# One transformer layer on one core: the last two value projections run among the first scores, probability buffers are numbered anew, and VectorE's third tile is taken at position 12

## The chip, the cores and the metric

The kernel runs on 1 core of one Trainium2 chip. The metric is the device time in microseconds of one execution. The times of the kernel before are 620.38 us median of 3 runs (620.07 to 620.94).

## What is computed

One layer in float32 on 2048 tokens of 256 channels: self-attention with 16 heads of 16 channels, a residual and a layer norm, then a gated feed-forward part with int8 weights, a residual and a second layer norm. Cut to what matters:

```python
Q = X @ Wq + bq; K = X @ Wk + bk; V = X @ Wv + bv           # 2048 x 256 each
scores = einsum('bhqd,bhkd->bhqk', q, k) / sqrt(16)         # 16 heads
attn = softmax(scores); out = einsum('bhqk,bhkd->bhqd', attn, v)
x = layernorm(X + out @ Wo + bo)
ffn = qmatmul(silu(qmatmul(x, w_gate, s_gate)) * qmatmul(x, w_up, s_up), w_down, s_down)
x = layernorm(x + ffn)
```

## The kernel before, in words

Every engine has its own hand-written list of instructions, and semaphores tie the lists together. Projections are done in three products of "high" and "low" parts, so that the result has nearly float32 precision.

**Projections.** TensorE (PE) turns X in four chunks of 512 tokens, projects queries and keys (`QK`, 16 tiles), and then values: `project_v(p)` for p = 0 to 7, each 12 matmuls of 256 columns for 256 tokens, into the PSUM bank `V_BANK[p]`. VectorE (DVE) copies each to `v_all` with the bias added (`save_v`, line 716). On its list `write_bound(0)` and `write_bound(1)` (line 737) stand among the eight `save_v`, and behind them the load of `exact_flag` (line 747) and a branch round a general path which these inputs don't need. PE (line 1129) and SyncE (SP, line 453) have the same load and branch.

**Attention** goes in 16 steps (4 chunks of 512 queries times 4 groups of 4 heads), each of 16 units, one for 128 keys. In unit u, PE runs `scores(2u)` and `scores(2u+1)` (line 1190: two matmuls each, 512 columns), and then `prob_times_v(u-2)` (line 1216: four matmuls, one for each head), so products run two units behind scores. Score pairs go round three pairs of PSUM banks, so `scores(g)` waits for the exponential of pair g-3. ScalarE (ACT) takes each pair as one exponential of 1024 columns (line 629) into `probs`, six buffers in turn (`g % HALVES`).

**Tiles taken by VectorE.** In a step, for some key tiles `kt` the exponential of head 0 is done by DVE with a polynomial (`exponentials`, lines 852 to 876, eight instructions), and ACT then takes only 512 columns of that pair. They are tiles 10 and 13 in step 1, and 2, 6, 10 and 13 in steps 2 to 15 (`poly_tiles`). Since DVE takes longer, head 0 multiplies such a tile later: `value_order` sets for each position of a step which tile head 0 takes there, while heads 1 to 3 take the tile of the position. Before, tile 10 is taken at position 13, and the ordinary tiles fill the positions between in their order, so that position 12 takes tile 14.

**What stands between.** In steps 5, 6, 9, 10, 13 and 14 PE runs `project_out` (line 1238, four matmuls) behind units 8 and 15; in steps 8 and 12 `turn_y` behind units 3 and 8.

**SP's queue** issues nearly all transfers: inputs, weights (`gate8`, `up8` and `down8` at lines 362 to 364), then `load_queries(0)`, the keys of step 0 (`load_k`), `load_queries(1)`, and `load_keys(1)` to `load_keys(3)` (lines 382, 384 and 392). Behind them come the flag, `load_queries(2)` with `load_shift` (line 406), and `move_out(0)`. DVE's first polynomial waits until the keys of steps 2 and 3 are loaded, since its buffers lie over `k_part`.

**Memory.** `probs` lies over `xt_hi` and the lower half of `xt_lo`, which the value projections read; `w_hi` and `w_lo`, with the value weights in them, lie over the keys of step 2.

Of the kernel before, what the change touches and what calls it, by code (L numbers as in the profile page):

```python
# [7 lines left out]
def layer_program(nc, X, Wq, bq, Wk, bk, Wv, bv, Wo, bo, w_gate, w_up, w_down, s_gate, s_up, s_down, out):  # L8
# [7 lines left out]
    P = 128  # L16
# [39 lines left out]
    with ExitStack() as ctx:  # L56
        arena_at = (nc.sbuf_base + 63) // 64 * 64
# [15 lines left out]
        KB = 1024  # L73

        x_tok = place("x_tok", [P, TT, HID], f32)
        gate8 = place("gate8", [P, KO, INTER // 4], i32)
        up8 = place("up8", [P, KO, INTER // 4], i32)
        down8 = place("down8", [P, MT, HID // 4], i32)
# [56 lines left out]
        w_hi = place("w_hi", [P, 3, KO, HID], f32r, at + 32 * KB)  # L135
        w_lo = place("w_lo", [P, 3, KO, HID], f32r, at + 38 * KB)
# [147 lines left out]
        V_BANK = [4, 5, 2, 3, 4, 5, 7, 6]  # L284
# [23 lines left out]
        def value_order(s):  # L308

            behind = {2: 5, 6: 9, 10: 13, 13: 15}  # L310
            late = {behind[kt]: kt for kt in poly_tiles(s)}
            others = [kt for kt in range(UPS) if kt not in poly_tiles(s)]
            return [late[i] if i in late else others.pop(0) for i in range(UPS)]

# [21 lines left out]
        def _(sp):  # L336
# [25 lines left out]
            sp.dma_start(gate8[:], w_gate.rearrange("(k p) n -> p k n", p=P)).then_inc(late_loaded, 16)  # L362
            sp.dma_start(up8[:], w_up.rearrange("(k p) n -> p k n", p=P)).then_inc(late_loaded, 16)
# [82 lines left out]
            sp.wait_ge(v_psum, TT // 2)  # L446
# [7 lines left out]
            with sp.If(need_exact > 0):  # L454
                sp.wait_ge(q_loaded[0], QUERY)
                for s in range(STEPS):

                    if s:
                        sp.wait_ge(gen_max, s * NQ * TPC + 2)
                    load_queries(s, 0, gen_loaded)  # L460
                sp.wait_ge(gen_max, STEPS * NQ * TPC + 2)
                load_queries(0, 0, gen_reloaded)

                sp.wait_ge(gen_split, 3)
                load_shift(0, 0, gen_reloaded)
# [108 lines left out]
        def _(act):  # L574
# [12 lines left out]
            def hi_of_w(i):  # L587
                act.wait_ge(w_loaded[i], 16)
                nc.scalar.copy(w_hi[:, i, :, :], w_raw[:, i, :].rearrange("p (k n) -> p k n", k=KO)
                               ).then_inc(w_hi_ready, 1)  # L590
# [75 lines left out]
        def _(dve):  # L666
# [14 lines left out]
            def lo_of_w(i):  # L681
                dve.wait_ge(w_hi_ready, i + 1)
                nc.vector.tensor_tensor(w_lo[:, i, :, :], w_raw[:, i, :].rearrange("p (k n) -> p k n", k=KO),
                                        w_hi[:, i, :, :].bitcast(f32), ALU.subtract).then_inc(w_ready, 1)
# [58 lines left out]
            for p in range(3, TT // 2):  # L743
                save_v(p)
# [3 lines left out]
            with dve.If(need_exact > 0):  # L748
# [28 lines left out]
                nc.vector.tensor_copy(shift[:, 1, :], shift_rest[:]).then_inc(gen_split, 1)  # L777

# [251 lines left out]
        def _(pe):  # L1030
# [69 lines left out]
            def project_v(p):  # L1100
# [4 lines left out]
                elif p in (4, 5):  # L1105

                    pe.wait_ge(v_ready, p - 3)
                elif p >= 6:

                    pe.wait_ge(norms_ready, 1)  # L1110
                for a in range(2):
# [4 lines left out]
                                    lambda ko: w_hi[:, 2, ko, :], lambda ko: w_lo[:, 2, ko, :])  # L1116
# [8 lines left out]
            for p in range(1, TT // 2):  # L1125
# [4 lines left out]
            with pe.If(need_exact > 0):  # L1130
# [6 lines left out]
                pe.wait_ge(v_ready, TT // 2)  # L1137
# [26 lines left out]
            def scores(g):  # L1164
# [15 lines left out]
                elif g < 3:  # L1180

                    pe.wait_ge(v_ready, 2 * (g + 1))
# [12 lines left out]
            def prob_times_v(u):  # L1195

                s, kt = u // UPS, u % UPS
                if u == 0:
                    pe.wait_ge(v_ones, 1)
                    pe.wait_ge(v_ready, TT // 2)  # L1200
# [9 lines left out]
                for hh in range(NQ):  # L1210
# [3 lines left out]
                    else:  # L1214
                        prob = probs[:, g % HALVES, hh % 2, :]
# [152 lines left out]
```

## Time and profile before

| | us |
|---|---|
| median of 3 runs | 620.38 (620.07 to 620.94) |
| the profiled execution's own time | 621.71 |
| its span in the trace | 619.9 |
| PE busy | 590.7 (95%) |
| ACT busy | 511.7 (83%) |
| DVE busy | 408.3 (66%) |
| GpSimd busy | 54.6 (9%) |
| mean granted TensorE clock | 0.992 of full |

The attention steps lie between 46.4 us and about 516 us of the span, the projections before them and most of the feed-forward part after them. A busy PE says little by itself: a matmul that is spread out counts as busy. The waits are read from the timeline, where a row in square brackets tells how long its engine stood idle before it and who released it.

### The profile page before, as it was taken

How to read it: one execution, taken by the hardware profiler on the slowest of the kernel's cores; microseconds unless marked ns; L12 is line 12 of the kernel's file. 1: busy time of each engine (PE TensorE's matmuls, PEld its weight loads, DVE VectorE, ACT ScalarE, POOL GpSimd, SP SyncE). 2: the span in 40 equal slices, each digit the busy share in tenths (PEclk: the TensorE clock that was granted, in tenths of full speed). 3: DMA queues.
4: the chain of work that ended last, by engine and by line, in shares of the span. 5: the costliest groups of instructions: out<-in, count | busy, mean ns of one | idle time of the engine just before them, and what ended most of it. 6: DMA issues, size and time to landing. Idle time of an engine off the chain costs nothing.

```text
span 619.9 us, 10436 instructions
## 1 busy us (share of the span) xinstructions
PE 590.7 (95%) x3952; PEld 248.7 (40%) x3952; DVE 408.3 (66%) x748; ACT 511.7 (83%) x614; POOL 54.6 (9%) x51
## 2 busy tenths in 40 slices
PE   8999999999999999999999999999999999999994
PEld 7892222222222222222222222222322226978874
DVE  7672005667676757597775658786766586777875
ACT  4628999999999999999998999999999996253352
POOL 7606000000000000000000000002000001102021
PEclk9997999999999999999999999999999999999998
DMA  9657882211112010101111111102010000101102
GB/s 222 117 94 101 121 107 34 34 27 17 28 13 62 10 30 7 31 7 33 45 30 17 21 22 18 27 11 63 10 30 9 5 7 7 40 1 34 35 1 68
DMA packets 36183, 24.69 MB, mean 40 GB/s; under 512 B 24930, under 2 KB 30946, under 8 KB 35538
## 3 DMA queue, kind: packets, MB, share of 16 engines
q1 hardware_dynamic: 34932, 23.42, 22.3%
q10 hardware_dynamic: 1200, 0.59, 0.4%
q8 instruction: 32, 0.52, 0.3%
q14 instruction: 19, 0.16, 0.1%
HBM read 6.56 MB, written 4.33 MB: 18 GB/s over the span
## 4 chain that ended last, share of the span: by engine, by line
PE 86%; ACT 8%; issue 3%; DVE 2%; DMA 1%; ACTq 0%; POOLq 0%; POOL 0%; DVEq 0%
PE ps L1216 37%; PE ps L1190 25%; PE ps L1321 10%; ACT probs L629 7%; PE ps L1063 5%; PE ps L1298 4%; PE ps L1238 3%; DMA x_tok<-in_L_attn_X 1%; DVE attn_q L784 1%; PE ps L1256 1%; PE ps L1049 1%; DVE stats L1005 0%; DVE r_tmp L1002 0%; DVE xt_lo L689 0%; DVE r_tmp L999 0%
## 5 line engine op out<-in xcount | busy, mean ns | idle before, releaser
L629 ACT ACTIVATE probs<-ps 128x1024 f32<-128x1024 f32 (+1 forms) x512 | 449.1, 1075 | 30.7 <-PE ps L1190 30.7
L1216 PE MATMUL ps<-probs,v_all 128*17 128x512 f32 x1932 | 270.6, 602 | 17.1 <-ACT probs L629 15.8
L1190 PE MATMUL ps<-q_slot,k_stack 51*128 51x512 f32 x1024 | 198.2, 459 | 1.5 <-ACT probs L629 1.5
L1190 PEld LDWEIGHTS ps<-q_slot,k_stack 51*128 51x128 f32 x1024 | 84.3, 185 | 222.7 <-ACT probs L629 209.7
L852 DVE TENSOR_SCALAR bits<-ps 128x512 int32<-128x512 f32 x58 | 40.0, 689 | 61.0 <-PE ps L1190 59.9
L784 DVE COPY attn_q<-ps 128x512 f32<-128x512 f32 x16 | 11.1, 691 | 91.9 <-PE ps L1216 91.9
L1216 PEld LDWEIGHTS ps<-probs,v_all 128*17 128x17 f32 x1932 | 33.6, 95 | 82.6 <-issue 49.0
L648 ACT ACTIVATE sg<-ps,sgate_c 128x512 f32<-128x512 f32 x32 | 22.1, 689 | 49.4 <-PE ps L1321 49.4
L1216 PE MATMUL ps<-poly,v_all 128*17 128x512 f32 x116 | 59.9, 598 | 0.0
L876 DVE SCALAR_TENSOR_TENSOR poly<-poly,bits 128x512 f32<-128x512 f32 x58 | 40.2, 692 | 6.0
L872 DVE SCALAR_TENSOR_TENSOR poly<-poly,mant 128x512 f32<-128x512 f32 x58 | 40.1, 692 | 2.0
L545 POOL TENSOR_TENSOR rstd<-var_eps,minus_half 128x4 f32<-128x4 f32 x4 | 4.1, 1029 | 420.6 <-DVE var_eps L820 420.6
L868 DVE SCALAR_TENSOR_TENSOR poly<-poly 128x512 f32<-128x512 f32 x58 | 39.7, 685 | 0.0
L863 DVE SCALAR_TENSOR_TENSOR poly<-mant 128x512 f32<-128x512 f32 x58 | 39.7, 685 | 0.0
L1321 PE MATMUL ps<-qy,wg 128*128 128x512 f32 x128 | 35.7, 400 | 0.0
L969 DVE SCALAR_TENSOR_TENSOR h<-ps,sup_c,sg 128x512 f32<-128x512 f32 x32 | 23.9, 747 | 16.2 <-ACT sg L648 16.2
L1321 PE MATMUL ps<-qy,wu 128*128 128x512 f32 x128 | 34.4, 390 | 0.0
L1298 PE MATMUL ps<-wd,h_hi 128*128 128x256 f32 x128 | 31.2, 285 | 0.0
L1298 PE MATMUL ps<-wd,h_lo 128*128 128x256 f32 x128 | 30.9, 283 | 0.0
L1321 PEld LDWEIGHTS ps<-qy,wu 128*128 128x128 f32 x128 | 24.0, 188 | 5.4
L858 DVE TENSOR_SCALAR bits<-bits 128x512 int32<-128x512 int32 x58 | 24.8, 428 | 2.0
L866 DVE TENSOR_SCALAR mant<-mant 128x512 f32<-128x512 f32 x58 | 24.8, 427 | 2.0
(97 smaller groups left out, 455.8 us busy)
## 6 DMA issues: line engine op xcount, KB each, us to landing
q_slot<-qy SPq DMA_DIRECT2D x64, 64.0 KB
k_stack<-k_part SPq DMA_DIRECT2D x12, 256.0 KB
at_dram<-attn_q SPq DMA_DIRECT2D x64, 34.0 KB
at<-at_dram SPq DMA_DIRECT2D x8, 272.0 KB, 3.0
q_slot<-qy SPq DMA_DIRECT2D x64, 32.0 KB
x_tok<-in_L_attn_X SPq DMA_DIRECT2D x14, 128.0 KB, 6.3
k_stack<-k_part SPq DMA_DIRECT2D x12, 128.0 KB
out<-out_tmp SPq DMA_DIRECT2D x12, 128.0 KB, 2.2
```

What stands on the lines that cost most here:

```text
L629: nc.scalar.activation(probs[:, g % HALVES, first:2, :].rearrange("p a b -> p (a b)"), ps[:, 2 * ring + first:2 * ring + 2, :].rearrange(" ...
L852: nc.vector.tensor_scalar(bits[:], ps[:, 2 * ring, :], TO_BITS, LOWEST, ALU.mult, ALU.max).then_inc(poly_read, 1)
L858: nc.vector.tensor_scalar(bits[:], bits[:], EXPONENT, BIAS, ALU.bitwise_and, ALU.bitwise_xor).then_inc(poly_exponent, 1)
L863: nc.vector.scalar_tensor_tensor(res, mant_f[:], POLY["a"], mant_f[:], ALU.add, ALU.mult).then_inc(poly_square, 1)
L868: nc.vector.scalar_tensor_tensor(res, res, POLY["b"], res, ALU.add, ALU.mult).then_inc(poly_square, 1)
L872: nc.vector.scalar_tensor_tensor(res, res, POLY["c"], mant_f[:], ALU.add, ALU.mult).then_inc(poly_cube, 1)
L876: nc.vector.scalar_tensor_tensor(res, res, POLY["d"], bits_f[:], ALU.add, ALU.mult).then_inc(poly_done, 1)
L1063: last = nc.tensor.matmul(dst, w(ko), x(ko), start=(n == 0), stop=(n == len(terms) - 1))
L1190: last = nc.tensor.matmul(ps[:, 2 * ring + half, :], k_stack[s % QUADS][base:base + ROWS, p, kt * P:(kt + 1) * P], q_slot[slot][base:base ...
L1216: last = nc.tensor.matmul(ps[32 * hh:32 * hh + VW, ACC, :], v_all[:, tiles[hh], NQ * (s % QUADS) + hh, :], prob, start=(kt == 0), stop=(kt ...
L1298: last = nc.tensor.matmul(ps[:, 4 + i, 0:HID], h[:, m, i * P:(i + 1) * P], wd[:, m, :], start=(m == 0 and j == 0), stop=(m == MT - 1 and j ...
L1321: last = nc.tensor.matmul(ps[:, bank, :], w[:, ko, m * P:(m + 1) * P], qy[:, c, ko, part, :], start=(ko == 0 and part == 0), stop=(ko == K ...
```

## The change

- `project_v(6)` runs between `scores(0)` and `scores(1)`, and `project_v(7)` behind `scores(3)` (the second pair of unit 1). ACT waits for six value projections before its first exponential in place of eight, and for all eight before its fourth (g = 3). `V_BANK` and the waits of the projections are changed to suit.
- DVE does `save_v(6)` and `save_v(7)` behind `write_bound(1)`, the flag and the branch.
- `probs` is used in the order of slots 0, 2, 4, 1, 3, 5, since the rows that `project_v(6)` and `project_v(7)` still read lie under slots 1, 3 and 5.
- The value weights' parts have a place of their own (`wv_hi`, `wv_lo`) over `gate8` and `up8`. These two loads (256 KB each) are moved on SP's queue from line 362 to behind the flag, ahead of `load_queries(2)`. `load_keys(2)` no longer waits for the value projections.
- In `value_order`, tile 10 goes to position 12.

```diff
-        V_BANK = [4, 5, 2, 3, 4, 5, 7, 6]
+        V_BANK = [4, 5, 2, 3, 4, 7, 6, 7]
+        V_LATE = 6
...
-            behind = {2: 5, 6: 9, 10: 13, 13: 15}
+            behind = {2: 5, 6: 9, 10: 12, 13: 15}
...
+        def slot_of(g):
+
+            return (0, 2, 4, 1, 3, 5)[g % HALVES]
...
-            sp.dma_start(gate8[:], w_gate.rearrange("(k p) n -> p k n", p=P)).then_inc(late_loaded, 16)
-            sp.dma_start(up8[:], w_up.rearrange("(k p) n -> p k n", p=P)).then_inc(late_loaded, 16)
...
             load_keys(1)
-            sp.wait_ge(v_psum, TT // 2)
             load_keys(2)
...
+            sp.wait_ge(v_psum, TT // 2)
+            sp.dma_start(gate8[:], w_gate.rearrange("(k p) n -> p k n", p=P)).then_inc(late_loaded, 16)
+            sp.dma_start(up8[:], w_up.rearrange("(k p) n -> p k n", p=P)).then_inc(late_loaded, 16)
             for s in range(STEPS):
...
-            act.wait_ge(v_psum, TT // 2)
+            act.wait_ge(v_psum, V_LATE)
...
                 act.wait_ge(scores_ready, g + 1)
+                if g == 3:
+                    act.wait_ge(v_psum, TT // 2)
...
-                    probs[:, g % HALVES, first:2, :].rearrange("p a b -> p (a b)"),
+                    probs[:, slot_of(g), first:2, :].rearrange("p a b -> p (a b)"),
...
-            for p in range(3, TT // 2):
+            for p in range(3, V_LATE):
                 save_v(p)
...
+            for p in range(V_LATE, TT // 2):
+                save_v(p)
...
-            for p in range(1, TT // 2):
+            for p in range(1, V_LATE):
                 project_v(p)
...
-                    pe.wait_ge(v_ready, 2 * (g + 1))
+                    pe.wait_ge(v_ready, 3 + g)
...
                     pe.wait_ge(v_ones, 1)
+                    pe.wait_ge(v_ready, V_LATE + 1)
+                elif u == 2 * (V_LATE + 1):
                     pe.wait_ge(v_ready, TT // 2)
...
                 scores(2 * u)
+                if u == 0:
+                    project_v(V_LATE)
                 scores(2 * u + 1)
+                if u == 1:
+                    project_v(V_LATE + 1)
```

How the lists of instructions move is shown at three places. The first is PE behind the branch, where `MATMUL ps<-q_slot,k_stack` is half a score pair and `ps<-wv_hi,xt_hi` and the like are the value projections. In the kernel before, the eight projections are over here:

```order
213 L1190 MATMUL ps<-q_slot_103,k_stack_92 128x512 [waits bound_ready,ones_ready,norms_ready,k_loaded0,q_loaded0]
214 L1190 MATMUL ps<-q_slot_103,k_stack_92 128x512
215 L1190 MATMUL ps<-q_slot_103,k_stack_92 128x512 [waits v_ready]
```

In the changed kernel:

```order
199 L1208 MATMUL ps<-q_slot_105,k_stack_94 128x512 [waits bound_ready,ones_ready,norms_ready,k_loaded0,q_loaded0]
200 L1208 MATMUL ps<-q_slot_105,k_stack_94 128x512
201 L1078 MATMUL ps<-wv_hi,xt_hi 128x256 [waits norms_ready]
...
207 L1078 MATMUL ps<-wv_hi,xt_lo 128x256 x2
208 L1208 MATMUL ps<-q_slot_105,k_stack_94 128x512 [waits v_ready]
...
212 L1208 MATMUL ps<-q_slot_105,k_stack_94 128x512 [waits exp_done]
213 L1208 MATMUL ps<-q_slot_105,k_stack_94 128x512
214 L1078 MATMUL ps<-wv_hi,xt_hi 128x256 [waits v_ready]
```

Twelve matmuls of a projection now stand behind the first score pair, and twelve more behind the fourth, which is the first one that waits for an exponential.

The second place is PE at the end of step 1: the product of position 12, the scores of unit 15, the product of position 13 (`poly` is a tile that DVE has done, `probs` one of ACT's). Before:

```order
393 L1216 MATMUL ps<-probs,v_all 17x512 [waits exp_done]
394 L1216 MATMUL ps<-probs,v_all 17x512 x3
395 L1190 MATMUL ps<-q_slot_104,k_stack_93 128x512 [waits exp_done]
...
399 L1216 MATMUL ps<-poly,v_all 17x512 [waits poly_done,exp_done]
400 L1216 MATMUL ps<-probs,v_all 17x512 x3
```

In the changed kernel:

```order
393 L1236 MATMUL ps<-poly,v_all 17x512 [waits poly_done,exp_done]
394 L1236 MATMUL ps<-probs,v_all 17x512 x3
395 L1208 MATMUL ps<-q_slot_106,k_stack_95 128x512 [waits exp_done]
...
399 L1236 MATMUL ps<-probs,v_all 17x512 [waits exp_done]
400 L1236 MATMUL ps<-probs,v_all 17x512 x3
```

DVE's tile and ACT's tile have changed places; the number of matmuls is the same.

The third place is SP's queue ahead of the queries of step 2, in the changed kernel:

```order
216 L460 UNCONDITIONAL_BRANCH [waits gen_reloaded]
217 L475 DMA gate_50<-in_L_ffn_w_gate 128x2x256 [waits v_psum]
218 L476 DMA up_51<-in_L_ffn_w_up 128x2x256
219 L378 DMA q_slot_105<-qy 32x1x512 [waits scores_ready]
```

Before, the load of the queries follows the branch directly, and the two weight loads stand ahead of all queries and keys.

## Rows read from the trace of the kernel before

**Rows 1.** The page's costliest groups, the exponentials: busy, mean ns, idle before

```profile
L629 ACT ACTIVATE probs<-ps 128x1024 f32<-128x1024 f32 (+1 forms) x512 | 449.1, 1075 | 30.7 <-PE ps L1190 30.7
```

**Rows 2.** Timeline of ACT: start us, length us, instructions, idle before and its releaser

```profile
46.96 5.61 ACT L629 ACTIVATE probs<-ps 128x1024 f32<-128x1024 f32 x6 [11.81 <-PE ps L1190]
53.27 1.94 ACT L629 ACTIVATE probs<-ps 128x1024 f32<-128x1024 f32 x2 [0.71 <-PE ps L1190]
56.26 48.77 ACT L629 ACTIVATE probs<-ps 128x1024 f32<-128x1024 f32 x54 [1.05 <-PE ps L1190]
105.69 27.73 ACT L629 ACTIVATE probs<-ps 128x1024 f32<-128x1024 f32 x32 [0.66 <-PE ps L1190]
...
208.82 10.31 ACT L629 ACTIVATE probs<-ps 128x1024 f32<-128x1024 f32 x12 [0.37 <-PE ps L1190]
...
222.50 15.84 ACT L629 ACTIVATE probs<-ps 128x1024 f32<-128x1024 f32 x18 [0.77 <-PE ps L1190]
...
513.00 1.94 ACT L629 ACTIVATE probs<-ps 128x1024 f32<-128x1024 f32 x2 [0.66 <-PE ps L1190]
```

**Rows 3.** Timeline of PE, end of step 1: position 12, scores of units 15 and 16

```profile
104.16 1.05 PE L1216 MATMUL ps<-probs,v_all 128*17 128x512 f32 x8 [1.10 <-ACT probs L629]
105.14 0.73 PE L1190 MATMUL ps<-q_slot,k_stack 51*128 51x512 f32 x4
106.79 0.74 PE L1190 MATMUL ps<-q_slot,k_stack 51*128 51x512 f32 x4
```

**Rows 4.** Timeline of DVE and PE, step 6: tile 10's first and last instruction, position 12

```profile
240.42 0.69 DVE L852 TENSOR_SCALAR bits<-ps 128x512 int32<-128x512 f32 x1 [2.95 <-PE ps L1190]
244.53 0.69 DVE L876 SCALAR_TENSOR_TENSOR poly<-poly,bits 128x512 f32<-128x512 f32 x1
248.15 1.05 PE L1216 MATMUL ps<-probs,v_all 128*17 128x512 f32 x8 [1.02 <-ACT probs L629]
```

**Rows 5.** Timeline of PE: an output projection in step 6

```profile
237.11 1.13 PE L1238 MATMUL ps<-wo,at 128*128 128x256 f32 x4
```

**Rows 6.** Timeline of PE: the first matmuls of `project_v(6)`, the first scores

```profile
43.39 0.40 PE L1063 MATMUL ps<-w_hi,xt_hi 128*128 128x256 f32 x2
46.36 0.96 PE L1190 MATMUL ps<-q_slot,k_stack 51*128 51x512 f32 x6
```

**Rows 7.** Timeline of DVE: `save_v(5)`, `write_bound(1)`, and the first polynomial

```profile
43.59 0.69 DVE L716 TENSOR_TENSOR v_all<-ps,bv_b 128x512 f32<-128x512 f32 x1 [0.16 <-PE ps L1063]
47.07 3.53 DVE L737 TENSOR_SCALAR q_slot<-q_slot,bound_neg 1x1024 fp32r<-1x1024 f32 x2
96.08 0.69 DVE L852 TENSOR_SCALAR bits<-ps 128x512 int32<-128x512 f32 x1 [14.41 <-PE ps L1190]
```

**Rows 8.** Instructions on `exact_flag`: duration ns min/median/max, first and last start us

```profile
L747 DVEq TENSOR_LOAD <-exact_flag x1: 548/548/548, 46.5 to 46.5; - x1
L453 SPq TENSOR_LOAD <-exact_flag x1: 2057/2057/2057, 89.9 to 89.9; - x1
```

**Rows 9.** Windows: us, busy (x instructions) of PE, PEld, DVE, ACT, POOL; granted clock; DMA

```profile
48.00:50.00 2.00, 1.13 (x6) 0.51 (x6) 1.97 (x2) 2.00 (x3) 2.00 (x2) 0.96 0.67 86
50.00:52.00 2.00, 2.00 (x10) 0.31 (x10) 0.61 (x1) 2.00 (x3) 2.00 (x3) 0.50 0.82 86
...
93.00:94.00 1.00, 1.00 (x10) 0.19 (x2) 0.00 (x0) 1.00 (x3) 0.00 (x0) 1.00 0.06 16
```

**Rows 10.** Timeline of SP's queue: a weight, step 0's last keys, step 2's queries and shifts

```profile
13.86 2.93 SPq L362 DMA_DIRECT2D gate<-in_L_ffn_w_gate  x1
...
40.35 0.59 SPq L384 DMA_DIRECT2D k_stack<-k_part  x1
...
92.81 0.61 SPq L371 DMA_DIRECT2D q_slot<-qy  x1
...
97.90 2.54 SPq L406 DMA_DIRECT2D q_slot<-shift  x4
```

**Rows 11.** DMA issues from 39 to 41 us: count, KB each, median us to landing

```profile
k_stack<-k_part SPq DMA_DIRECT2D x2, 32.0 KB, 2.0
```

More of the change, by code:

```diff
@@ L56, in layer_program @@
     with ExitStack() as ctx:
+        KB = 1024
         arena_at = (nc.sbuf_base + 63) // 64 * 64
@@ L71, in region @@
             return at
-        KB = 1024
         x_tok = place("x_tok", [P, TT, HID], f32)
+        at = place_at[0]
         gate8 = place("gate8", [P, KO, INTER // 4], i32)
         up8 = place("up8", [P, KO, INTER // 4], i32)
+        wv_hi = place("wv_hi", [P, KO, HID], f32r, at)
+        wv_lo = place("wv_lo", [P, KO, HID], f32r, at + 2 * KB)
         down8 = place("down8", [P, MT, HID // 4], i32)
@@ L134, in layer_program @@
         squares = place("squares", [P, 4, S], bf16, at + 16 * KB)
-        w_hi = place("w_hi", [P, 3, KO, HID], f32r, at + 32 * KB)
-        w_lo = place("w_lo", [P, 3, KO, HID], f32r, at + 38 * KB)
+        w_hi = place("w_hi", [P, 2, KO, HID], f32r, at + 32 * KB)
+        w_lo = place("w_lo", [P, 2, KO, HID], f32r, at + 36 * KB)
         wg = place("wg", [P, KO, INTER], f32r, at)
@@ L588, in hi_of_w @@
                 act.wait_ge(w_loaded[i], 16)
-                nc.scalar.copy(w_hi[:, i, :, :], w_raw[:, i, :].rearrange("p (k n) -> p k n", k=KO)
+                nc.scalar.copy(w_hi[:, i, :, :] if i < 2 else wv_hi[:], w_raw[:, i, :].rearrange("p (k n) -> p k n", k=KO)
                                ).then_inc(w_hi_ready, 1)
@@ L682, in lo_of_w @@
                 dve.wait_ge(w_hi_ready, i + 1)
-                nc.vector.tensor_tensor(w_lo[:, i, :, :], w_raw[:, i, :].rearrange("p (k n) -> p k n", k=KO),
-                                        w_hi[:, i, :, :].bitcast(f32), ALU.subtract).then_inc(w_ready, 1)
+                hi, lo = (w_hi[:, i, :, :], w_lo[:, i, :, :]) if i < 2 else (wv_hi[:], wv_lo[:])
+                nc.vector.tensor_tensor(lo, w_raw[:, i, :].rearrange("p (k n) -> p k n", k=KO), hi.bitcast(f32),
+                                        ALU.subtract).then_inc(w_ready, 1)
             def lo_of_x(c):
@@ L1104, in project_v @@
                     pe.wait_ge(lo_ready, NQK - 3 + p - 0)
-                elif p in (4, 5):
-                    pe.wait_ge(v_ready, p - 3)
-                elif p >= 6:
+                elif p == 4:
+                    pe.wait_ge(v_ready, 1)
+                elif p in (5, 6):
                     pe.wait_ge(norms_ready, 1)
+                elif p == 7:
+                    pe.wait_ge(v_ready, 6)
                 for a in range(2):
@@ L1115, in project_v @@
                                     lambda ko: xt_lo[:, ko, t * P:(t + 1) * P],
-                                    lambda ko: w_hi[:, 2, ko, :], lambda ko: w_lo[:, 2, ko, :])
+                                    lambda ko: wv_hi[:, ko, :], lambda ko: wv_lo[:, ko, :])
                 last.then_inc(v_psum, 1)
@@ L1136, in _ @@
                     pe.wait_ge(k_loaded[quad], keys_of(quad))
-                pe.wait_ge(v_ready, TT // 2)
+                pe.wait_ge(v_ready, V_LATE)
                 pe.wait_ge(norms_ready, 2)
@@ L1214, in prob_times_v @@
                     else:
-                        prob = probs[:, g % HALVES, hh % 2, :]
+                        prob = probs[:, slot_of(g), hh % 2, :]
                     last = nc.tensor.matmul(ps[32 * hh:32 * hh + VW, ACC, :],
```

## The prediction

> **What bounds the kernel now.** I read the page's costliest groups first. The exponentials on ACT are busy for 449.1 us and idle 30.7 us before them, always for PE's scores [rows 1]. 11.8 us of this is the wait for the first one, so some 19 us of idle time lie inside the attention steps. ACT's timeline shows where [rows 2]: it starts at 46.96, is idle 0.71 and 1.05 us in the first eight exponentials, then runs without a break until 105, and from there has a break of 0.66 us once in each step, 15 times from 105.69 to 513.00. Breaks of 0.77 us follow six of these at once (the one at 222.50 is shown), and six of 0.37 to 0.38 us stand in the middle of a step (208.82). The sum is 1.76 + 9.9 + 4.6 + 2.3, and two of 0.2: 19 us, so nothing is missing.
>
> One exponential takes 0.92 us from start to start: (5.61 - 1.94) / 4 [rows 2]. A step with its four half exponentials keeps ACT for 27.73 us. PE needs 106.79 - 105.14 = 1.65 us a unit [rows 3], 26.4 us for 16. So a step is bound by ACT, and each of its breaks is paid in full, as long as PE can use its 1.3 us of room. In steps with two projections of 1.1 us [rows 5] PE needs 28.6 us, and ACT 27.73 + 0.37 + 0.4 = 28.5 if the large break shrinks to the size of the small one: there the two are level.
>
> **Tile 10 at position 12.** At the end of step 1 PE stands idle 1.10 us before the product of position 12, released by ACT [rows 3]. By the lists it takes tile 14 there for head 0, and the scores of tile 14 were issued immediately ahead of it, in the same unit: it waits for an exponential that has just been asked for. Only behind it come the scores of unit 15 at 105.14, and ACT's break ends at 105.69. With tile 10 there, PE needs only a polynomial. Tile 14 goes to position 13, one unit later, behind scores that wait for the same exponential anyway. The same pattern stands in all 15 steps with polynomials: 15 x 0.66 = **-9.9 us**.
>
> Is tile 10 ready? In step 6 its chain begins at 240.42 and ends at 245.22 [rows 4]. PE came to position 12 at 248.15 - 1.02 = 247.13. That is 1.9 us of room. DVE had been idle 2.95 us before the chain, so nothing pushes it.
>
> A projection behind unit 15 now comes right after the stall and costs ACT 0.77 us, one behind unit 8 has no stall ahead and costs 0.37 [rows 2]. Without the stall both should cost alike: 6 x 0.40 = **-2.4 us**. The bounds are 0 (PE is level with ACT there) and 4.6; I take the row for unit 8, which is the same work in the same steps.
>
> **Projections 6 and 7 among the scores.** Projection 6 starts at 43.39 and scores at 46.36 [rows 6]: two projections take 2.88 us. First scores now start at 43.48, if their data are there. The last keys of step 0 are issued at 40.35 [rows 10] and land 2.0 us later [rows 11], at 42.4: in time by 1.1 us. ACT starts 0.60 us behind the scores, at 44.08. Projection 6 (1.44 us) then stands ahead of the second pair: that pair comes at 45.34, ACT sees it at 45.94, idle 0.94 us. Pairs 2 and 3 follow until 46.6, projection 7 ends at 48.1, and the fourth exponential waits for it: the third ended at 47.8, idle 0.4 us. PE has work without a break until then and ACT is fed with three pairs at once, so the breaks of 0.71 and 1.05 us [rows 2], which came while PE waited and then ran slowly, go. Start: -2.88 + 0.94 + 0.4 - 1.76 = **-3.3 us**.
>
> The clock is part of it. PE was busy 1.13 of 2.00 us in the window at 48, and the next has a granted clock of 0.50, that is 1.2 GHz [rows 9]. The Trainium skill ("TensorE: Matmul & The Clock Gate", Part 1) says that half rate is the default and activity lifts it. The trace agrees with the fall. By that rule alone one may fear that the smaller matmuls and waits of the new start still drop it; this is rival D.
>
> DVE now does `save_v(6)` behind `write_bound(1)`, the flag and the branch, and the first product (about 48.9) waits for it. `save_v(5)` ends at 44.28 [rows 7]. The two bounds took 3.53 us beside GpSimd's additions; now they come before those. At worst 44.28 + 3.53 + 0.69 = 48.5, still in time; the flag's load takes 0.55 us on DVE's queue and was done while the engine was at other work [rows 8]. Even if it stood in line with SP's 2.06 us, the first product would be 1.6 us late, which I keep for the range. The move of `save_v(7)` is free: its first reader is unit 14. Renaming the slots moves no work: **0**, covered by the wait of g = 3 that I have counted.
>
> **The weight loads on SP's queue.** This term goes the other way. SP issues the keys of steps 1 to 3 without a pause and reads the flag at 89.9, in 2.06 us [rows 8]. Queries of step 2 start at 92.81, the last shift is issued at 97.90 + 2.54 = 100.44 [rows 10]. Nothing of this chain starts earlier when attention does. Two issues are put ahead of it; on a quiet queue I price them at 0.61 each, like the query's issue at 92.81 (DMA busy 0.06 in 93 to 94 [rows 9]), so 1.2 us, and the queries land at 101.64 + 2.0 = 103.6. They are wanted earlier: pair 64 went to ACT at 105.69 + 1.84 = 107.53, and now could at 107.53 - 0.66 - 3.3 = 103.57, with scores 0.60 us ahead, at 102.97. Loss: **+0.6 us**. Bounds: 0 and rival B. The gap at the input's end of the queue (13.86) hid behind queries that were not yet wanted, so it gives nothing.
>
> DVE's first polynomial waits for the keys of step 3. DMA engines are quiet from 93.0 [rows 9]; the polynomial began at 96.08 [rows 7] and may now begin at 92.8. This is even, 0 to 0.7 us, and it falls in front of the wait for queries, which would swallow it: 0. Everything behind the attention steps is as before; the weights for GpSimd's casts are wanted hundreds of us later.
>
> **Sum:** -9.9 - 2.4 - 3.3 + 0.6 = -15.0 us. The profiled execution took 621.71 us (span 619.9), 1.3 above the median of 620.38. Against its own time this gives 606.7, and for a median **605.4 us**.
>
> **Rivals.**
>
> - **B, the weight loads hold the queue.** If both issues take 2.93 us, as `gate` did at 13.86 [rows 10], they cost 5.9 and not 1.2: the queries land 4.7 us later and PE waits all of it at the head of step 2. 605.4 + 4.7 = 610.1 us. For it: a full queue has made issues this long. Against: the DMA engines have just gone quiet. The Trainium skill ("Trainium Kernel Development and Optimization", Key Constraints) says that all queues share the same 16 DMA engines and interleave; by that, 512 KB ahead of the queries slow them too. That speaks against the change, and no row of before shows it at this place.
> - **C, the stall only moves to position 13.** Then the 9.9 and 2.4 us stay, and the start alone is won: 620.4 - 2.7 = 617.7 us, and no change within the measurement if the start fails too. Against it: at position 13 PE has already waited for that exponential in the scores of unit 15.
> - **D, the clock falls all the same at the start.** The 1.76 us of breaks come back, the wait for queries goes: -9.9 - 2.4 - 1.5, 606.6 us.
> - **E, slower.** The polynomial of tile 10 isn't ready at position 12. Its price is paid in every step from 1.9 us of lateness on, and the kernel is slower once it is some 3.4 us late. If one more chain of 4.8 us stands ahead of it, PE waits 2.9 us, ACT 2.45 in place of 0.66: 15 x 1.79 - 5.1 = +21.8, 642 us. For it: DVE does norms and copies between the tiles in steps 4 to 15. Against: 2.95 us of idle time ahead of the chain [rows 4].
>
> **Numbers.** The forecast (A) gets 0.75, B 0.10, C 0.05, D 0.06, E 0.03, anything else 0.01. A's own bounds are -0.6 (no wait for queries) and -1.6 more (projections cost less than 0.37) below, +2.4 (no gain there) and +1.6 (late `save_v(6)`) above: 603.2 to 609.4 us. This holds A nearly whole, D, and a B with one long issue, 0.8 in all, and so is the range. Under 0.2% (1.2 us) a measurement of this kernel can't tell from no change. Faster by more: A, B, D and most of C, 0.95; within: the rest of C, 0.02; slower: E, 0.03.
>
> **What would show it.** ACT's first exponential at about 44.1; the breaks of 0.66 us gone from its timeline, a step of 27.8 us in place of 28.4, and those of 0.77 near 0.4; position 12 with `poly` and no wait; granted clock 1.00 from 46 to 58; the queries of step 2 issued from about 94.0, and one PE wait of under 1 us at the head of step 2. The prediction is wrong if a break of over 0.4 us stands in each step behind position 12 or 13, if `gate` and `up` take more than 2 us to issue, or if ACT's ninth exponential (at 56.26 before) starts later than 54.

## The result, and the profile after

The changed kernel takes **605.82 us** (median of 4 runs, 604.9 to 608.15), the kernel before, run beside it on the same chip, 620.66 us (620.07 to 621.45). The ratio is 0.9766 (95% interval 0.9734 to 0.9798). Predicted were 605.4 us and a range of 603.2 to 609.4. The profiled execution took 604.9 us with a span of 603.1; the one of before had a span of 619.9. Between the two profiles lie 16.8 us, between the medians 14.8; the difference between these two numbers is part of what follows. One slow execution of the kernel before, of 708.61 us at a mean granted clock of 0.751, belongs to the third set below and is left out of every comparison.

| | before | after |
|---|---|---|
| span of the profile, us | 619.9 | 603.1 |
| PE busy | 590.7 (95%) | 591.0 (98%) |
| ACT busy | 511.7 | 510.2 |
| exponentials: busy, idle before | 449.1, 30.7 | 447.6, 15.0 |
| first exponential | 46.96 | 44.05 |
| granted TensorE clock | 0.992 | 0.998 |

The page's group of exponentials after the change (busy, mean ns, idle before), which answers to [rows 1]:

```profile
L640 ACT ACTIVATE probs<-ps 128x1024 f32<-128x1024 f32 (+1 forms) x512 | 447.6, 1113 | 15.0 <-PE ps L1208 14.6
```

And ACT's timeline, which answers to [rows 2] (start, length, instructions, idle before and its releaser):

```profile
44.05 1.03 ACT L640 ACTIVATE probs<-ps 128x1024 f32<-128x1024 f32 x1 [8.55 <-PE ps L1208]
45.98 1.94 ACT L640 ACTIVATE probs<-ps 128x1024 f32<-128x1024 f32 x2 [0.90 <-PE ps L1208]
48.10 48.27 ACT L640 ACTIVATE probs<-ps 128x1024 f32<-128x1024 f32 x53 [0.17 <-PE ps L1078]
96.57 105.59 ACT L640 ACTIVATE probs<-ps 128x1024 f32<-128x1024 f32 x122 [0.21 <-PE ps L1208]
202.54 12.14 ACT L640 ACTIVATE probs<-ps 128x1024 f32<-128x1024 f32 x14 [0.37 <-PE ps L1208]
215.12 15.84 ACT L640 ACTIVATE probs<-ps 128x1024 f32<-128x1024 f32 x18 [0.44 <-PE ps L1208]
...
357.13 71.44 ACT L640 ACTIVATE probs<-ps 128x1024 f32<-128x1024 f32 x82 [0.45 <-PE ps L1208]
...
498.15 1.28 ACT L646 ACT_TABLE_LOAD   x1
```

The break of 0.66 us that stood in each step is gone: one row of 122 exponentials now runs past four of its places. The six of 0.77 us are 0.43 to 0.45, and the six of 0.37 stand as they were. The two of 0.20 us behind `turn_y` no longer show (the row at 357.13 runs through step 12, where one stood before); whether they were a gain is looked at further down. ACT is done with the attention steps at 498.15; before, its last exponentials began at 513.00 and took 1.94. That is 16.8 us earlier, the whole difference of the spans, so nothing behind the attention steps changed.

Position 12 of step 1 is the place that [rows 3] showed. On PE's timeline it is now:

```profile
99.32 0.73 PE L1208 MATMUL ps<-q_slot,k_stack 51*128 51x512 f32 x4
99.99 0.60 PE L1236 MATMUL ps<-poly,v_all 128*17 128x512 f32 x1
99.99 0.62 PE L1236 MATMUL ps<-probs,v_all 128*17 128x512 f32 x3
```

The product takes `poly` and follows the scores without a wait; before, 1.10 us of idle time stood ahead of it.

The start, on PE's timeline (of each projection the first row alone):

```profile
43.45 0.50 PE L1208 MATMUL ps<-q_slot,k_stack 51*128 51x512 f32 x2
43.87 0.51 PE L1078 MATMUL ps<-wv_hi,xt_hi 128*128 128x256 f32 x2
...
45.45 0.96 PE L1208 MATMUL ps<-q_slot,k_stack 51*128 51x512 f32 x6
46.34 0.51 PE L1078 MATMUL ps<-wv_hi,xt_hi 128*128 128x256 f32 x2
...
47.93 0.73 PE L1208 MATMUL ps<-q_slot,k_stack 51*128 51x512 f32 x4
48.59 1.05 PE L1236 MATMUL ps<-probs,v_all 128*17 128x512 f32 x8
```

A projection behind the first pair, three pairs at once, the other projection, and from there scores and products in turn, with no row that waits. The windows show the clock (us, busy time and instructions of PE, PEld, DVE, ACT, POOL; granted clock; DMA's share and GB/s); [rows 9] has the same two windows of before, with 0.96 and 0.50:

```profile
48.00:50.00 2.00, 2.00 (x15) 0.55 (x14) 0.69 (x1) 1.90 (x3) 2.00 (x3) 1.00 0.19 31
50.00:52.00 2.00, 1.98 (x16) 0.58 (x14) 0.00 (x0) 2.00 (x4) 2.00 (x2) 1.00 1.07 127
```

### The profile page after: what moved, and what is told of

It reads as the page before. It is cut to its first block, busy times and chain, and to the rows that moved or that the text cites. A ratio compares the mean times of both kernels' runs of the same rounds, so it can differ in the third digit from the quotient of the medians.

```text
span 603.1 us, 10438 instructions
## 1 busy us (share of the span) xinstructions
PE 591.0 (98%) x3952; PEld 249.9 (41%) x3952; DVE 407.5 (68%) x748; ACT 510.2 (85%) x614; POOL 54.4 (9%) x51
## 4 chain that ended last, share of the span: by engine, by line
PE 95%; DVE 2%; ACT 1%; DMA 1%; issue 1%; ACTq 0%; POOLq 0%; POOL 0%; DVEq 0%
PE ps L1236 41%; PE ps L1208 29%; PE ps L1345 10%; PE ps L1078 6%; PE ps L1322 4%; PE ps L1258 3%; DMA x_tok<-in_L_attn_X 1%; ACT probs L640 1%; DVE attn_q L799 1%; PE ps L1276 1%; PE ps L1064 1%; DVE stats L1020 0%; DVE r_tmp L1017 0%; DVE xt_lo L701 0%; DVE r_tmp L1014 0%
## 5 line engine op out<-in xcount | busy, mean ns | idle before, releaser
L640 ACT ACTIVATE probs<-ps 128x1024 f32<-128x1024 f32 (+1 forms) x512 | 447.6, 1113 | 15.0 <-PE ps L1208 14.6
L1208 PE MATMUL ps<-q_slot,k_stack 51*128 51x512 f32 x1024 | 201.2, 461 | 0.5 <-ACT probs L640 0.4
L891 DVE SCALAR_TENSOR_TENSOR poly<-poly,bits 128x512 f32<-128x512 f32 x58 | 41.6, 718 | 6.0
```

The source lines that it names most:

```text
L640: nc.scalar.activation(probs[:, slot_of(g), first:2, :].rearrange("p a b -> p (a b)"), ps[:, 2 * ring + first:2 * ring + 2, :].rearrange(" ...
L891: nc.vector.scalar_tensor_tensor(res, res, POLY["d"], bits_f[:], ALU.add, ALU.mult).then_inc(poly_done, 1)
L1208: last = nc.tensor.matmul(ps[:, 2 * ring + half, :], k_stack[s % QUADS][base:base + ROWS, p, kt * P:(kt + 1) * P], q_slot[slot][base:base ...
```

## The experiments

Ten kernels ran. "Before" and "changed" name the kernel from which an edit starts; kernels of one set share their runs of the kernel before, whose median was 620.3 us in the first set, 621.17 in the second and 621.36 in the third.

### The two parts apart

**Order only:** the kernel before with tile 10 at position 12.

```diff
-            behind = {2: 5, 6: 9, 10: 13, 13: 15}
+            behind = {2: 5, 6: 9, 10: 12, 13: 15}
```

> The kernel before with tile 10 at position 12 and nothing else. My theory: the 15 breaks of 0.66 us go (-9.9) and six of 0.77 shrink to 0.44 (-2.0), while the first breaks of 0.71 and 1.05 us and the granted clock of 0.50 after 50 us stay as before: 608 to 609 us. Rival, the stall only moves to position 13: 620 us. Rival, the early start is needed for this gain (PE's room comes from there): 612 us or more.

Measured: 608.29 us (606.96 to 608.78, 4 runs), ratio 0.9801 (0.978 to 0.9821). **Start only:** the changed kernel with that line set back.

> The changed kernel with tile 10 back at position 13. My theory: the first exponential at 44.05 us, breaks of 0.90 and 0.17 us behind it, the breaks of 0.66 us back: 616.5 to 617.5 us (-3.4 us against before, less 0 to 0.3 for the first polynomial, which waits for the keys of step 3). Rival, the keys or the queries of step 2 swallow the early start: 619 us or more. The two parts should add: gains of this run and of the order alone sum up to that of the change within 0.5 us, unless the clock differs.

Measured: 619.08 us (618.45 to 623.48, 10 runs), ratio 0.9989 (0.9971 to 1.0006).

So the order is worth 12.0 us by medians and the start 1.2: 13.2 together, while both have 14.8 in the first comparison. The start's 1.2 is not clear of nothing in this run alone, since the interval of its ratio reaches from 0.9971 to 1.0006; it also misses what I expected (616.5 to 617.5) and lies where the rival put it (619 or more). ACT's timeline of the order alone:

```profile
47.11 5.61 ACT L629 ACTIVATE probs<-ps 128x1024 f32<-128x1024 f32 x6 [11.80 <-PE ps L1190]
53.41 1.94 ACT L629 ACTIVATE probs<-ps 128x1024 f32<-128x1024 f32 x2 [0.70 <-PE ps L1190]
56.38 149.12 ACT L629 ACTIVATE probs<-ps 128x1024 f32<-128x1024 f32 x170 [1.03 <-PE ps L1190]
```

From the ninth exponential on there is no break in 149 us, but the two breaks of the start are still there. The start alone shows the opposite: ACT's first row at 44.01, the new start's own breaks of 0.96 and 0.16 in place of 0.7 and 1.0, and 0.66 in every step:

```profile
48.09 47.34 ACT L640 ACTIVATE probs<-ps 128x1024 f32<-128x1024 f32 x52 [0.16 <-PE ps L1078]
95.78 1.02 ACT L640 ACTIVATE probs<-ps 128x1024 f32<-128x1024 f32 x1 [0.34 <-PE ps L1208]
97.19 5.23 ACT L640 ACTIVATE probs<-ps 128x1024 f32<-128x1024 f32 x6 [0.39 <-PE ps L1208]
103.08 27.73 ACT L640 ACTIVATE probs<-ps 128x1024 f32<-128x1024 f32 x32 [0.66 <-PE ps L1208]
```

The row at 103.08 stood at 105.69 before [rows 2]: the start has won 2.6 us against the profiled execution of before. It had won more. The ninth exponential starts at 52.6 (five of 0.91 us behind the row at 48.09), 3.6 us earlier than at 56.26. From there to the break at the end of step 1 ACT took 48.77 us before and takes 49.8 here, so 1.0 us is lost again. Two new breaks, 0.34 and 0.39, stand on this stretch, at 95.78 and 97.19. I had given this place 0.3 us at most; the experiment on the weight loads below turns to it. The rest of the miss lies in what the 3.4 us were counted against, which the next experiments show.

### Where 1.6 us hide: the clock at the start

The missing 1.6 us led to the runs of the kernel before. In the second set they fall into two groups: mean granted clocks of 0.991 to 0.993 with 621.0 to 622.5 us, and 0.995 to 0.997 with 620.06 to 620.33 (one run of 621.48 stands apart). The profiled execution, 621.71 us at 0.992, is like the first group. Its 6.83 us at half clock from 49.8 on make 0.5 x 6.83 / 619.9 = 0.0055, about the difference between the groups. So the fall of the clock would come in some executions of before and not in others; over all three sets, 20 of the 34 compared executions of before have a mean clock of 0.994 or less. The test fills PE's idle time there: 17 transposes (8 + 3 + 3 + 3; the expectation below calls them fourteen), whose result nobody reads, in the first units of the kernel before.

```diff
+            def filler(count):
+                pe.wait_ge(v_ready, 7)
+                for _ in range(count):
+                    nc.tensor.transpose(ps[:, 7, 0:P], ident[:], ident[:])
...
                 scores(2 * u)
+                if u in (1, 2):
+                    filler(8 if u == 1 else 3)
                 scores(2 * u + 1)
+                if u in (1, 2):
+                    filler(3)
```

> The kernel before with fourteen extra transposes into a free bank among the scores of units 1 and 2, where PE waits for the first exponentials (they compute nothing that is used). My theory on the clock: the fall to 0.50 after 50 us follows PE's idle time there and costs 1.76 us of breaks, in some of the runs; with PE busy it doesn't fall: every run at 619.8 to 620.3 us with a clock of 0.995 or more, none at 621 to 622. Rival, the clock falls for another reason: times and clocks spread as in the kernel before (0.991 to 0.998, 619.9 to 622.3 us).

Measured: 620.35 us (619.91 to 620.97, 10 runs), ratio 0.9986 (0.9974 to 0.9997). All ten runs have a clock of 0.995 to 0.997, and none is slower than 621 us, against 621.17 as the median of before in the same set. (Six of the ten lie above the 620.3 us that I had set as their upper end, by up to 0.7.) ACT's timeline has one row from the first exponential on where [rows 2] has three:

```profile
47.51 56.15 ACT L629 ACTIVATE probs<-ps 128x1024 f32<-128x1024 f32 x62 [11.80 <-PE ps L1190]
104.32 27.73 ACT L629 ACTIVATE probs<-ps 128x1024 f32<-128x1024 f32 x32 [0.66 <-PE ps L1190]
```

and the windows are

```profile
48.00:50.00 2.00, 2.00 (x15) 1.34 (x14) 1.97 (x2) 2.00 (x3) 2.00 (x2) 1.00 0.31 48
50.00:52.00 2.00, 2.00 (x14) 0.94 (x16) 0.19 (x1) 2.00 (x3) 2.00 (x2) 1.00 1.14 127
```

With PE busy 2.00 of 2.00 us from 46 to 50, in place of 1.13 in the window at 48 [rows 9] and of 1.32 in the one ahead of it,

```profile
46.00:48.00 2.00, 1.32 (x10) 0.71 (x8) 1.53 (x2) 1.04 (x2) 2.00 (x2) 1.00 0.50 82
```

the clock stays at 1.00. The Trainium skill ("TensorE: Matmul & The Clock Gate", Part 1) calls half rate the default that activity lifts; the two pairs of windows agree. More work on PE made the kernel 0.8 us faster here. Idle time does not bring the fall every time: in the kernel with the old buffer numbers, below, PE is busy 0.86 and 1.54 us in the windows at 48 and 50, and its profiled execution keeps 1.00.

**Order and filler:** the last kernel with tile 10 at position 12 as well. If the missing part is the clock alone, the parts must now add up.

> The kernel before with the third VectorE tile at position 12 and, in the first units, 14 transposes whose result nobody reads between TensorE's scores, so that it has no idle time there. Theory: the two parts of the change add up, and what is missing between them (12.0 of the order, 1.2 of the start, against 14.8 to 15.6 of both) is the half clock near 50 us, which the order alone keeps in most of its runs. Then this kernel shows no half clock at 50, ScalarE's breaks of 0.7 and 1.0 us near 53 and 56 are gone, and its time is about 606.9 (606.5 to 607.4, ratio 0.978). The rival, that the parts help one another in another way (the order alone worth 12.0 whatever the clock), expects 608.3 as for the order alone.

Measured: 606.74 us (605.87 to 606.81, 5 runs), ratio 0.9763 (0.9745 to 0.978). ACT runs from the start to the first projection without any break, and then has the projections' alone:

```profile
47.47 156.51 ACT L629 ACTIVATE probs<-ps 128x1024 f32<-128x1024 f32 x178 [11.80 <-PE ps L1190]
204.35 12.14 ACT L629 ACTIVATE probs<-ps 128x1024 f32<-128x1024 f32 x14 [0.37 <-PE ps L1190]
```

The ladder is then 620.35 (no idle time), 606.74 (order too), 605.56 (the change, run again below): the order is worth **13.6 us** and the new start **1.2**, the same 1.2 as alone. The second rung comes from another set than the other two; the kernel with the weight loads moved, in the same set as it, has 605.48. The theory's 606.9 holds, the rival's 608.3 does not. The traces give the same for the order without any median: from the ninth exponential to the last, ACT took 514.94 - 56.26 = 458.7 us before and 501.49 - 56.38 = 445.1 with the order alone, both with the half clock ahead of this stretch, so 13.6. By medians the order alone shows less, and the clocks fit that: all four of its runs have 0.994 or less, and only six of the thirteen of before beside it. Against an undisturbed start the row of this kernel at 204.35 answers to the changed kernel's at 202.54: 1.8 us between the two profiled executions.

### The buffer numbers

The changed kernel with slots in plain order. What `project_v(7)` reads then lies under the second slot, so the wait for all projections has to come at g = 1.

```diff
-            return (0, 2, 4, 1, 3, 5)[g % HALVES]
+            return g % HALVES
...
-                if g == 3:
+                if g == 1:
```

> The changed kernel with the old numbers of the probability buffers, so that the second exponential (its buffer lies over rows that projection 7 still reads) waits for all eight value projections, in place of the fourth. My theory: the second exponential starts at 48.1 in place of 46.0, two exponentials (1.84 us) later than now, PE waits for them and the whole attention moves: +1.5 to +1.9 us against the changed kernel, unless the key loads had held the changed kernel (then 0.2 us less). Rival, the start is paid back at the keys of step 3 or the queries of step 2 anyway: +0.5 us or less.

Measured: 607.03 us (606.63 to 607.65, 4 runs), ratio 0.9783 (0.9766 to 0.9799).

```profile
44.91 1.03 ACT L640 ACTIVATE probs<-ps 128x1024 f32<-128x1024 f32 x1 [8.55 <-PE ps L1208]
48.96 50.10 ACT L640 ACTIVATE probs<-ps 128x1024 f32<-128x1024 f32 x55 [3.02 <-PE ps L1078]
```

One break of 3.02 us takes the place of 0.90 and 0.17, and the time is 1.5 us above the changed kernel's of the second set. That is as long as the order without the new start (606.74), so without the numbering the new start wins nothing that these runs show: it moves no work, but it decides how many exponentials may run ahead of the last projection.

### How much room tile 10 has

**The changed kernel again**, as the measure for its neighbours.

> The changed kernel itself, beside the others of this batch. Expected 605 to 606 us, 1.5 us under the run with the old numbers, with a granted clock of 0.996 or more; runs of over 606.5 us should be those with a lower clock (0.994). If it comes out at 607.3 us like the split projections, these cost nothing and gain nothing, and the first measurement of the change was 1.5 us low.

Measured: 605.56 us (605.33 to 606.47, 4 runs), ratio 0.9752 (0.973 to 0.9775). **Tile 10 at position 11:**

```diff
-            behind = {2: 5, 6: 9, 10: 12, 13: 15}
+            behind = {2: 5, 6: 9, 10: 11, 13: 15}
```

> The changed kernel with tile 10 one position earlier still, at 11. It tests the room that the third tile has: at position 12 I read 1.9 us between the end of its chain and PE's arrival; one unit less leaves 0.2 us. If the room is what I read: 0 to 2 us slower than the changed kernel, with small waits of PE for DVE at position 11 in the steps in which DVE is busiest. If the chain has less room than I read, a wait of over 0.5 us in each of 15 steps: 5 us slower or more.

Measured: 606.04 us (605.32 to 606.91, 4 runs), ratio 0.9752 (0.973 to 0.9775), the same time. Waits of PE for VectorE's tiles, in all 15 steps together:

```profile
DVE poly L891: 0.3, 1
```

One wait of 0.3 us, in the first step with a polynomial. Position 12 therefore has one unit of room more than it needs, and rival E had no ground.

### The projections' breaks

Twelve breaks of 0.37 to 0.45 us are left, behind each `project_out`. **Split:** each projection in two halves, behind units 8 and 9, 14 and 15.

```diff
-                if c >= 0 and stage in (1, 2) and kt in (8, 15):
-                    project_out(c, 2 * (stage - 1) + kt // 15)
+                if c >= 0 and stage in (1, 2) and kt in (8, 9, 14, 15):
+                    project_out(c, 2 * (stage - 1) + kt // 14, (0,) if kt in (8, 14) else (1,))
```

> The changed kernel with each output projection of steps 5, 6, 9, 10, 13 and 14 cut in two halves of two matmuls, behind units 8 and 9 and behind units 14 and 15, in place of four matmuls at once. If the breaks of 0.37 and 0.44 us that are left are caused by the burst of 1.1 us, they go: -3 to -4.9 us against the changed kernel. If PE is simply full in these steps (28.6 us of work against 27.8 us of ACT), the breaks are only spread out: 0 to -1 us. I expect the second.

Measured: 607.31 us (607.15 to 607.46, 4 runs), ratio 0.979 (0.9774 to 0.9807). The breaks of a step are now

```profile
204.35 8.66 ACT L640 ACTIVATE probs<-ps 128x512 f32<-128x512 f32 x10 [0.34 <-PE ps L1208]
213.20 1.94 ACT L640 ACTIVATE probs<-ps 128x1024 f32<-128x1024 f32 x2 [0.19 <-PE ps L1208]
215.47 17.72 ACT L640 ACTIVATE probs<-ps 128x1024 f32<-128x1024 f32 x20 [0.34 <-PE ps L1208]
```

0.87 us in place of 0.81 by the brackets: a burst cut in two leaves as much idle time in more pieces. It costs more than the brackets say. From this step's first projection to the next step's, ACT takes 233.53 - 204.35 = 29.18 us, and 231.34 - 202.54 = 28.80 in the changed kernel. The 0.38 more in each of six steps is 2.3 us, all that lies between the two spans (605.4 and 603.1; 1.5 to 1.8 by medians). I had expected 0 to 1 us less than the changed kernel, and 3 to 4.9 less if the burst is the cause: both missed. **Moved:** the fourth projection behind unit 3 of the next step, where none stood.

```diff
-                if c >= 0 and stage in (1, 2) and kt in (8, 15):
+                if c >= 0 and stage in (1, 2) and kt in (8, 15) and (stage, kt) != (2, 15):
                     project_out(c, 2 * (stage - 1) + kt // 15)
+                if c >= 0 and stage == 3 and kt == 3:
+                    project_out(c, 3)
```

> The changed kernel with the last of the four output projections moved from unit 15 of steps 6, 10 and 14 to unit 3 of steps 7, 11 and 15, where PE has 1.4 us of room. If PE is full in the steps with two projections, three breaks of 0.44 us go and nothing comes: -1.3 us against the changed kernel. If the breaks come from the burst of 1.1 us, they only change their place: 0.

Measured: 605.43 us (604.68 to 609.17, 4 runs), ratio 0.9759 (0.9716 to 0.9801).

```profile
251.99 64.45 ACT L640 ACTIVATE probs<-ps 128x1024 f32<-128x1024 f32 x74 [0.60 <-PE ps L1208]
```

Three breaks of 0.44 became three of 0.60 at the new place, although the step it left now has only one projection. So the break comes from the burst: 1.13 us of projection between two score pairs, at each of the three places tried, and not from the sum of PE's work in the step. The prediction reached the right size by both arguments and could not tell them apart; this run can, and it speaks against my sum of PE's time over a step (28.6 against 28.5) as the reason. Neither edit beats the change.

### The weight loads

The two loads moved behind the queries of step 2. (They keep their two semaphores; only their place in SP's queue is another.)

```diff
             sp.wait_ge(v_psum, TT // 2)
-            sp.dma_start(gate8[:], w_gate.rearrange("(k p) n -> p k n", p=P)).then_inc(late_loaded, 16)
-            sp.dma_start(up8[:], w_up.rearrange("(k p) n -> p k n", p=P)).then_inc(late_loaded, 16)
...
                 move_out(s)
+                if s == 2:
+                    sp.dma_start(gate8[:], w_gate.rearrange("(k p) n -> p k n", p=P)).then_inc(late_loaded, 16)
+                    sp.dma_start(up8[:], w_up.rearrange("(k p) n -> p k n", p=P)).then_inc(late_loaded, 16)
```

> The changed kernel with one edit: the loads of the gate and up weights are issued behind the queries of step 2 instead of ahead of them. The theory is that the two issues (0.40 + 0.46 us on SP's queue) only bring TensorE to the edge of the shifts of step 2, and that there is no break on ScalarE to win: the queries' first issue comes about 0.85 us earlier (near 92.5), TensorE's weight load of pair 64 no longer waits for the shifts, and the time stays at 605.6 (605.0 to 606.2, ratio 0.975). The rival, that the loads cost what the prediction's sum gave them, expects 605.0 or less with a break on ScalarE gone near 97; a second rival, that the weights' transfer then lies beside the queries' and delays them, expects 606.5 or more.

Measured: 605.48 us (604.26 to 606.17, 4 runs), ratio 0.9741 (0.9719 to 0.9764): the same time. In the changed kernel SP's queue reads

```profile
92.44 0.40 SPq L475 DMA_DIRECT2D gate<-in_L_ffn_w_gate  x1
92.89 0.46 SPq L476 DMA_DIRECT2D up<-in_L_ffn_w_up  x1
93.39 0.62 SPq L378 DMA_DIRECT2D q_slot<-qy  x1
```

The issues take 0.40 and 0.46 us where 0.61 each was assumed and 2.93 feared. The queries start at 93.39, and the scores of pair 64 follow at 102.62 without a wait. What `gate` took at 13.86 was no measure of such a load even before: the like load of `up`, right behind it, took 0.47.

```profile
16.83 0.47 SPq L363 DMA_DIRECT2D up<-in_L_ffn_w_up  x1
```

The Trainium skill's rule that all queues share the 16 DMA engines ("Trainium Kernel Development and Optimization", Key Constraints), on which rival B leaned, cost nothing that these two runs show.

In the run without the two issues the queries start at 93.50, and not near 92.5 as I expected: the last key is issued later there (89.54, against 88.70 in the changed kernel), so the two traces don't give the price of the issues by themselves.

The same run settles the two small breaks near 95. Without the weight loads they are still there, and larger than in the changed kernel's profile: PE's scores and DVE's first polynomial,

```profile
95.40 0.50 PE L1209 MATMUL ps<-q_slot,k_stack 51*128 51x512 f32 x2 [1.07 <-DVE bits L868]
...
94.57 0.69 DVE L868 TENSOR_SCALAR bits<-ps 128x512 int32<-128x512 f32 x1 [16.33 <-DMA k_stack<-k_part]
```

and in the changed kernel

```profile
93.78 0.69 DVE L867 TENSOR_SCALAR bits<-ps 128x512 int32<-128x512 f32 x1 [15.70 <-DMA k_stack<-k_part]
```

Before, the first polynomial began at 96.08 and waited for PE [rows 7]; now it waits for the keys of step 3, whose loads fill SP's queue from 47 us on. What is late next is thus that transfer, and not the weights. In all eight profiles with the new start it begins 4.0 to 4.4 us behind the end of the last key's issue:

```profile
88.70 1.04 SPq L391 DMA_DIRECT2D k_stack<-k_part  x1
...
89.54 0.90 SPq L391 DMA_DIRECT2D k_stack<-k_part  x1
```

(the changed kernel, this kernel). ACT's breaks there are 0.21 us in the changed kernel, 0.39 in its second run, and two of 0.73 together in the start alone and in this one. What they cost is more: over exponentials 49 to 94 the changed kernel takes 0.5 us longer than the two kernels with the new order and the old start, its second run 0.7, this kernel 1.1, the one with the moved projection 1.2. Tile 10 at position 11 takes 1.6, with its wait for the polynomial in it. Why the same chain of loads ends up to 1.7 us apart in these kernels (first polynomial at 93.75 to 95.43 where the buffers have their new numbers) stays open.

## Why the prediction was right, step by step

| step | predicted, us | measured, us |
|---|---|---|
| tile 10 at position 12 | -9.9 | 15 breaks of 0.66 gone (-9.9), and 0.11 with each (-1.6) |
| projection behind unit 15 | -2.4 | -2.0 (0.77 to 0.44, six) |
| `turn_y` | not named | -0.1 |
| the start, clock in it | -3.3 | -1.2 by medians, keys in it |
| keys of step 3 | 0 (0 to 0.7) | 0.5 to 1.2, inside the row above |
| weight loads and queries | +0.6 | 0 |
| sum | -15.0 | -14.8 by medians (-16.8 profile to profile) |

**The order.** The mechanism was right in each part: the stall was the wait for tile 14's exponential, PE had the room, and the polynomial was ready. Its size was 0.11 us too small in each step. An exponential that runs alone takes 1.03 us (44.05) and adds 0.92 in a row of others, since each begins before the last one has ended; a break takes this overlap away as well. One sees it in the copies that end each step, on DVE's timeline:

```profile
133.79 0.69 DVE L799 COPY attn_q<-ps 128x512 f32<-128x512 f32 x1 [3.42 <-PE ps L1236]
161.41 0.69 DVE L799 COPY attn_q<-ps 128x512 f32<-128x512 f32 x1 [3.41 <-PE ps L1236]
```

A step takes 161.41 - 133.79 = 27.62 us. Before it took 134.08 - 105.69 = 28.39 [rows 2], so 0.77 was won where the bracket showed 0.66. It also stands in ACT's busy time, which fell by 1.5 us with the same 512 exponentials. The breaks behind `turn_y` warn of the opposite error. Between the projections of steps 6 and 9, with two large breaks and one of 0.20 among 82 exponentials, the rows read

```profile
252.38 25.98 ACT L629 ACTIVATE probs<-ps 128x1024 f32<-128x1024 f32 x30 [0.77 <-PE ps L1190]
...
307.86 17.59 ACT L629 ACTIVATE probs<-ps 128x1024 f32<-128x1024 f32 x20 [0.66 <-PE ps L1190]
...
243.92 71.46 ACT L640 ACTIVATE probs<-ps 128x1024 f32<-128x1024 f32 x82 [0.44 <-PE ps L1208]
```

before (first two) and after (last): 307.86 + 17.59 - 252.38 = 73.07 us, and 71.46. Of the 1.61 us won, 1.54 are two steps of 0.77, so the break of 0.20 that vanished gave 0.07: it is 0.13 now, too short for the timeline to show. With it the order is worth 9.9 + 1.6 + 2.0 + 0.1 = 13.6, what the ladder measured.

**The projections.** "Without the stall both should cost alike" gave 0.37; they cost 0.44. The term was near (2.0 of 2.4), its second reason, that PE would be level with ACT over the step, fell.

**The start.** The times were met: first exponential predicted 44.08, measured 44.05 (43.91 to 44.91 in the other profiles with the new start, so that 0.03 us is closer than one trace can tell); the next break 0.94 and 0.90; the one for projection 7 0.4 and 0.17. `save_v(6)` went at 45.81, since the two bounds took 1.51 us and not 3.53, and the first product at 48.59 did not wait. The step that was wrong is the one that turned this into a median. The sum was made against the profiled execution, and the 1.3 us between it and the median were carried along as if they were spread over the kernel. The filler kernel shows what they are: without the half clock and the 1.76 us of breaks its span is 618.6 us, 1.3 less than 619.9, and by their mean clocks 14 of 34 executions of before had no such fall either. Against an undisturbed start the term was -2.88 + 0.94 + 0.4 = -1.5, and -1.2 was measured, after 0.5 to 1.2 us had been lost again to the keys.

**SP's queue.** The +0.6 did not come, for two reasons: the issues were 0.36 us shorter together than assumed, and the shifts were there soon enough for pair 64. The keys of step 3 took 0.5 to 1.2 instead, partly over the bound of 0.7, and were not hidden behind the queries as the prediction had it.

The errors of the sum have both signs. The gain was put 1.6 us too low for the overlap, 0.1 for `turn_y` and 0.6 for the queries, and too high by 2.1 us for the start and 0.4 for the projections; together they leave 0.2. The cause and the place of each gain were right, but that 605.4 lies 0.4 us from the median is luck: two errors of 1.6 and 2.1 us cancelled. Rival C is refuted by the timeline, rival D by the windows at 50 us, rival B by the rows at 92.44, rival E by the kernel with position 11.

## What to carry to other kernels

When an instruction waits for a result that was asked for immediately ahead of it, look for work of equal size that is ready, and swap the two; what it is worth is the period of the loop on the bounding engine before and after, which is more than the idle time in brackets when its instructions overlap, and can be less when a bracket only falls out of sight. Make the sum against the executions that the median stands for: where the profiled one is slower than the median, find the place of the difference before you count the repair of that place as a gain. And when a start moves earlier, every chain that does not move with it (here the keys on SP's queue) comes closer to being the next wait.

## What was not expected of the hardware

- The half clock (0.50, that is 1.2 GHz) at the start is a matter of the execution, with the same kernel and inputs: 6.83 us of it in the profile of before, and by their mean clocks in 20 of 34 executions. It follows 4 us in which PE was busy 2.45. With the 17 transposes, all fifteen runs of two kernels have 0.995 or more. With the new start single executions are still low: 0.994 with 608.15 us, 0.994 with 609.17, 0.947 with 623.48. No trace shows where.
- The same two bounds on DVE took 1.51 us at 44.27, ahead of GpSimd's additions, and 3.53 beside them [rows 7], 2 us longer; in three other profiles with the old start they took 2.56 to 3.46.
- A load of queries that otherwise issues in 0.59 us on SP's queue took 1.56 at 44.37 in the changed kernel, and one between 44.0 and 45.3 took 1.18 to 1.75 in each of the seven other profiles with the new start; in the four with the old one, none there did:

```profile
43.73 0.59 SPq L378 DMA_DIRECT2D q_slot<-qy  x1
44.37 1.56 SPq L381 DMA_DIRECT2D q_slot<-qy  x1
45.97 0.59 SPq L378 DMA_DIRECT2D q_slot<-qy  x1
```

The keys of step 1 are then issued from 47.32, in place of 46.15. What holds the queue there, and whether the keys of step 3 would come earlier without it, was not tried.
